# Three attentions with row maxima: the first group's keys and queries are loaded in two halves, and its row scores run by halves

## The reference

```python
scores = jnp.einsum('bhqd,bhkd->bhqk', wq, wk) * scale
scores = jnp.where(mask[None, None], neg, scores)
attn = jax.nn.softmax(scores, axis=-1)
outs.append(jnp.einsum('bhqk,bhkd->bhqd', attn, wv))
```

## Time and profile before

| | us |
|---|---|
| median of 3 runs | 2514.82 (2509.34 to 2515.09) |
| the profiled execution | 2509.64 |
| its span | 2507.9 |
| PE busy | 2108.8 (84%) |
| DVE busy | 1603.6 (64%) |
| ACT busy | 1412.7 (56%) |

### The profile page before, as it was taken

The page is one execution under the profiler, slowest core; times in us unless marked ns, Lnnn a source line. Parts: engine busy times, 40 slices in busy tenths (PEclk is TensorE's granted clock), DMA queues, the critical chain, the costliest instruction groups (busy, mean ns, idle before and its releaser), DMA issues. The chain is left out here.

```text
span 2507.9 us, 37005 instructions
## 1 busy us (share of the span) xinstructions
PE 2108.8 (84%) x13722; PEld 1249.1 (50%) x13732; DVE 1603.6 (64%) x3493; ACT 1412.7 (56%) x2024; POOL 781.3 (31%) x426
## 2 busy tenths in 40 slices
PE   4999999999999935758737786999979746999798
PEld 2666666666666522612323543444446633444367
DVE  5887787887877556631256655877623686877324
ACT  3777776777777643269752343466653152566541
POOL 3787776877877401142101203100000022000000
PEclk8999999999999966879958897799989876999999
DMA  2000000000000050062050211311010003110100
GB/s 75 1 5 1 3 5 1 1 3 5 1 3 1 1 172 0 17 159 53 1 172 1 73 45 46 83 40 40 2 34 1 1 8 90 50 40 21 35 1 18
DMA packets 43908, 82.10 MB, mean 33 GB/s; under 512 B 8962, under 2 KB 17810, under 8 KB 40722
## 3 DMA queue, kind: packets, MB, share of 16 engines
q1 hardware_dynamic: 43730, 79.74, 11.4%
HBM read 64.09 MB, written 14.88 MB: 31 GB/s over the span
## 5 line engine op out<-in xcount | busy, mean ns | idle before, releaser
L800 ACT ACTIVATE probs<-psum_banks 128x1024 f32<-128x1024 f32 (+1 forms) x416 | 381.3, 979 | 249.2 <-PE psum_banks L670 154.0
L1231 POOL TENSOR_SCALAR l0a_rows<-l0a_rows,l0a_rinv 128x1024 f32<-128x1024 f32 x160 | 454.8, 2847 | 188.0 <-DVE l0a_rinv L1193 184.2
L879 DVE TENSOR_REDUCE neg_max<-psum_banks 128x1 f32<-128x512 f32 (+3 forms) x672 | 406.1, 659 | 155.7 <-PE psum_banks L702 96.5
L1181 DVE TENSOR_REDUCE l0a_nmax<-psum_banks 128x1 f32<-128x1024 f32 x256 | 312.5, 1221 | 140.1 <-PE psum_banks L1075 138.2
L1127 ACT ACTIVATE l0a_rows<-psum_banks,l0a_nmax 128x1024 f32<-128x1024 f32 x256 | 286.0, 1117 | 60.6 <-DVE l0a_nmax L1181 59.3
L666 PE MATMUL psum_banks<-q_stack,k_stack 75*128 75x512 bf16 (+7 forms) x1216 | 277.0, 338 | 50.1 <-ACT probs L800 23.7
L698 PE MATMUL psum_banks<-k_stack,q_stack 72*128 72x128 bf16 (+3 forms) x1024 | 246.3, 325 | 46.4 <-DMA q_stack<-q_parts 41.8
L1089 PE MATMUL psum_banks<-packed,l0a_rows 128*128 128x128 f32 x2048 | 267.1, 273 | 2.0 <-POOL l0a_rows L1231 0.9
L1074 PE MATMUL psum_banks<-l0a_kh,l0a_qw 128*128 128x512 f32 x512 | 242.7, 474 | 21.4 <-POOL l0a_qw L1220 13.5
L1089 PEld LDWEIGHTS psum_banks<-packed,l0a_rows 128*128 128x128 f32 x2048 | 239.1, 141 | 42.4 <-issue 4.8
L686 PE MATMUL psum_banks<-probs,v_ones 128*32 128x512 f32 (+3 forms) x2432 | 238.8, 504 | 10.3 <-ACT o_sum L771 6.5
(11 more groups left out here) (289 smaller groups left out, 3516.5 us busy)
## 6 DMA issues: line engine op xcount, KB each, us to landing
q_stack<-q_parts SPq DMA_DIRECT2D x24, 576.0 KB
k_stack<-k_parts SPq DMA_DIRECT2D x48, 192.0 KB
qkv<-in_l0f_w SPq DMA_DIRECT2D x6, 1024.0 KB, 5.6
moe_b<-in_l0f_b SPq DMA_DIRECT2D x32, 128.0 KB, 3.7
k_stack<-k_eight SPq DMA_DIRECT2D x16, 256.0 KB
l1f_w<-in_l1f_w SPq DMA_DIRECT2D x16, 256.0 KB, 4.5
q_stack<-q_parts SPq DMA_DIRECT2D x32, 96.0 KB
q_parts<-parts SPq DMA_DIRECT2D x12, 256.0 KB
```

The lines of the kernel that those rows point to most:

```text
L800: act.activation(S.Pt[:, U % PBUFS, 2 * half:2 * half + 2, c0:HALF], PS[:, bank:bank + 2, c0:HALF], ACT.Exp).then_inc(exp_done, 1)
L879: dve.tensor_reduce(out, scores, AX, ALU.max, negate=True).then_inc(job_read, 1)
L1181: dve.tensor_reduce(R.nmax4[:, s % 4:s % 4 + 1], scores(s), AX, ALU.max, negate=True).then_inc(max_done, 1)
L1231: rows_divided.mark(pool.tensor_scalar(R.Pr[:, s % RING, :], R.Pr[:, s % RING, :], R.rinv4[:, s % 4:s % 4 + 1], None, ALU.mult))
```

## The change

In the three attentions with maxima, group 0 alone is loaded in two halves, heads 0 and 1, then heads 2 and 3: eight transfers of half the size instead of four. The first four count on a new semaphore, `half_landed`, the other four on `loaded`. The rows jobs of group 0 that came first are sorted, stably, so that all of heads 0 and 1 stand ahead of all of heads 2 and 3. The first job waits for `half_landed`; each job of group 0 that starts with head 2 waits for `loaded`. All other groups and all other jobs stay as they are. The whole diff:

```diff
--- before.py
+++ after.py
@@ -476,6 +476,7 @@
 
 def side_jobs(ng, nu, nk, use_max, lead):
 
+
     steps = [[] for _ in range(ng * nu + LAG + 5)]
 
     def spread(events, s0, n):
@@ -486,6 +487,8 @@
         first, second = row_jobs(nk)
         for g in range(ng):
             jobs = [("rows", g, job) for job in first + second]
+            if g == 0:
+                jobs = sorted(jobs[:len(first)], key=lambda e: e[2][1][0] >= 2) + jobs[len(first):]
             whole = ("turn", g, (0, 1))
             s0 = 1 + (g - lead) * nu
             if g >= lead and not second:
@@ -565,10 +568,10 @@
     for U in range(total):
         visits.append(visits[-1] + (1 if narrow(U) else 2))
 
-    with phase(S, 25) as (block, sems):
+    with phase(S, 26) as (block, sems):
         (cols_ready, exp_done, masked, pv_done, evicted, job_ready, job_read, split_done, c_split, c_copied,
          summed, part_done, rest_done, zeroed, v_ready, ones_set, stored) = sems[:17]
-        loaded, c_loaded = sems[17:21], sems[21:25]
+        loaded, c_loaded, half_landed = sems[17:21], sems[21:25], sems[25]
 
         def spare(e, w):
             return PS[:, ring[number[e] % len(ring)], 0:w]
@@ -599,12 +602,14 @@
                     for r0, parts in ((0, 3), (24, 3), (48, 2)):
                         sp.dma_start(S.Qst[64 * i + r0:64 * i + r0 + HD8 * parts, at, :],
                                      S.q_parts[b, 0:parts, :, heads, :].rearrange("j d h t -> (j d) h t")).then_inc(loaded[g % SLOTS], 16)
-                if use_max:
-                    k_rows = short_keys(S, b, keys)[:, :, h0:h0 + 4, :].rearrange("d j h t -> (d j) h t")
-                    q_rows = S.q_parts[b, :, :, h0:h0 + 4, :].rearrange("j d h t -> (j d) h t")
+                for i0, i1 in () if not use_max else ((0, 2), (2, 4)) if g == 0 else ((0, 4),):
+                    landing = half_landed if i1 == 2 else loaded[g % SLOTS]
+                    at, heads = slice(slot(g, i0), slot(g, i1 - 1) + 1), slice(h0 + i0, h0 + i1)
+                    k_rows = short_keys(S, b, keys)[:, :, heads, :].rearrange("d j h t -> (d j) h t")
+                    q_rows = S.q_parts[b, :, :, heads, :].rearrange("j d h t -> (j d) h t")
                     for copy in range(3):
-                        sp.dma_start(S.Kst[24 * copy:24 * (copy + 1), at, :], k_rows).then_inc(loaded[g % SLOTS], 16)
-                    sp.dma_start(S.Qst[0:72, at, :], q_rows.unsqueeze(1).to_broadcast([24, 3, 4, T])).then_inc(loaded[g % SLOTS], 16)
+                        sp.dma_start(S.Kst[24 * copy:24 * (copy + 1), at, :], k_rows).then_inc(landing, 16)
+                    sp.dma_start(S.Qst[0:72, at, :], q_rows.unsqueeze(1).to_broadcast([24, 3, i1 - i0, T])).then_inc(landing, 16)
 
             def load_c(e):
                 k, g, sides = turn_at[e], e[1], e[2]
@@ -690,7 +695,9 @@
 
             def scores(e):
                 _, g, (kind, heads, j) = e
-                if number[e] == 0 or order[number[e] - 1][:2] != ("rows", g):
+                if number[e] == 0:
+                    pe.wait_ge(half_landed, per_group)
+                elif order[number[e] - 1][:2] != ("rows", g) or (g == 0 and heads[0] == 2):
                     pe.wait_ge(loaded[g % SLOTS], per_group * (g // SLOTS + 1))
                 bank = spare(e, HALF)
 
```

## The result

| | before | changed |
|---|---|---|
| median of 8 runs each, us | 2513.0 | 2505.96 |
| lowest and highest | 2509.34, 2517.32 | 2503.04, 2508.49 |
| ratio, with its 95% interval | | 0.9967 [0.9956, 0.9978] |
| profiled execution, span, us | 2507.9 | 2505.2 |

The changed kernel is faster, by 0.33% as the ratio has it (8.3 us; its interval runs from 5.5 to 11 us) and by 7.0 us, 0.28%, between the medians. The time is inside the forecast range, and the gain a little more than the forecast 6.3 us. The 0.3% that I had drawn as the limit of "no change" lies between the two figures.

What follows compares the result with a forecast made beforehand. PE, busy 84%, was taken as the bound, idling at each attention's start for the queries' transfer. Gains of 3.5 us in two causal attentions less 0.7 windowed gave 6.3 us, from 2514.82 to 2508.5, range 2501 to 2515.

Steps and rivals of the forecast that it cites:

- First half in the causal attentions: Start of each causal attention: half the amount lands sooner, so PE starts 3.5 us earlier.
- all move by the same amount: Causal attentions: maxima, turn, shift, group 1's load and first columns move with step 0's jobs; 3.5 us gained each.
- rival 3 of the prediction: Causal attentions, chance 0.1: clock rises only after the next value products, up to 5.6 us more each; 4.9 us slower, 2519.7.
- Second half hidden: Causal attentions: seven jobs of heads 0 and 1, 4.2 us, cover the second half's landing; stall 0 to 0.5 us.
- Rival 4: Start of the attentions, chance 0.08: a stall before heads 2 and 3 loses the whole gain; 2514.8 us.
- rival 1: Group 0's loads, chance 0.2: halves less than half as fast, PE stalls at the eighth job; 3.3 us gained, 2511.5.
- New order free: Group 0's row scores: sorting the same 14 jobs by heads costs 0.
- The windowed attention: First attention: PE starts about 1.5 us earlier, but groups 1 to 3 issue 1.9 us later; cost 0.7 us.
- rival 2: Windowed attention, chance 0.22: group 0's turn comes earlier and loads catch up, gaining 1.5 us there; 8.9 us altogether, 2505.9.
- The sum: Whole kernel: 7.0 us from two causal attentions less 0.7 in the windowed one, 6.3 us, 0.25%.
- The rule weighed: Loads: the skill's fit, 2.0 us plus bytes at 436 GB/s per transfer, gives 1.3 us per causal attention, 1.9 overall.
- the signs that I had named for "wrong": PE waiting over 2 us amid step 0; clock rising elsewhere than after first values; stages after the attentions changing length.

Runs made afterwards that it cites:

- ones last: Changed kernel with the rows of ones issued behind the loads of groups 1 to 3 in the windowed attention; 2503.77 us against 2513.09 before, ratio 0.9956.
- causal, ones last: Changed kernel with halves in the causal attentions alone and the ones issued last in the windowed one; 2505.37 us against 2513.09 before, ratio 0.9967.
- ACT's queue: Changed kernel with the windowed attention's groups 1 to 3 issued from ACT's queue instead of behind group 0 on SP's; 2503.7 us against 2512.62 before, ratio 0.9958.
- keys whole: Changed kernel, windowed attention only: ones issued behind groups 1 to 3, group 0's keys whole, only its queries halved; 2504.43 us against 2513.09 before, ratio 0.9962.

## Why the prediction held, point by point

**First half in the causal attentions: right, a little small.** Forecast 3.5 us each, bounds 2.5 and 3.7. The lengths of the second attention's stage (to the mixture weights), and how much earlier than before PE starts in it:

| kernel | earlier start | shorter stage |
|---|---|---|
| changed | 4.37 | 4.17 |
| changed, again | 4.77 | 4.69 |
| causal only | 3.53 | 3.54 |
| causal only, again | 4.13 | 3.85 |
| ones last | 4.20 | 4.25 |
| causal, ones last | 4.19 | 3.79 |
| ACT's queue | 4.33 | 4.42 |
| keys whole | 1.88 | 1.06 |
| halves without the order | 4.54 | 1.32 |

The stage shrinks by what PE starts earlier, to within 0.4 us in all but the last two rows. The step "all move by the same amount" was right, and the last row is the exception that I had named: without the new order the start is as early and the gain is gone.

What the stage follows in every row is the rise of the clock. It comes 47.2 us after the first load before the change, 42.5 to 43.8 in the first seven rows, 47.0 with the keys whole and 46.0 without the order. In all 22 causal stages without a fall, halved or not, the stage is 238.9 to 240.3 us longer than the time to the rise. With the keys whole the first value product came 1.9 us earlier than before (43.50 for 45.40), but the clock still rose at 47.0, and of 1.88 us 1.06 were left. So the gain depends on the rise moving with the start, as rival 3 of the prediction has it; with halves and the new order it did in all but this row. In the third attention the six profiles without a fall of the clock are 3.45 to 4.14 us shorter with PE 3.46 to 4.27 earlier. Over all 14 stages with halves, the new order and no fall the mean is 3.7 us; with the two falls counted in, it is 3.0. The bound of 3.7 was too low: ten of the 16 stages started earlier by more. The starts scatter, from 5.5 to 6.8 us and once 8.43, and I could not see that from one profile of before, whose two starts lie 0.3 us apart.

**Second half hidden: right.** Forecast landing about 10.2 us after the first issue and at most 0.5 us of stall. It lands at 9.63 and 10.34 in the kernel that waits for it, and at the eighth job of the changed kernel there is no wait. Rival 4 and rival 1, which had a stall there, fell.

**New order free: right.** 286.99 and 286.65, against 286.97 and 286.63.

**The windowed attention: right in kind and place.** PE starts after 5.17 us (forecast 5.5), waits for group 1 until 1423.82 (forecast 1422.9 to 1423.9), the shift isn't earlier, and rival 2 fell with that. Forecast cost 0.7 us, bounds -1.5 and +1.9. At the first columns it is 20.54, 20.77 and 21.18 in three profiles with halves, mean 20.83, against 20.18, 19.78, 20.39, 20.06 and 20.36 in five without, mean 20.15: 0.7 us. The whole stage costs a little more: 139.78, 139.63 and 140.96, mean 140.1, against 139.11, 138.44, 139.28, 139.02 and 139.35, mean 139.0. For the other 0.4 there is a candidate that I had not foreseen. During the wait for group 1 the granted clock falls. The timeline has PE idle for 2.95 us until 1423.82, and in the windows of the changed kernel shown above the clock is at 1.00 in 1421 to 1422, at 0.71 in the next microsecond, at 0.50 when PE starts again, and still there in 1428 to 1429. The earlier trace rows had 1.00 in both of its microseconds. In the five profiles without halves the clock didn't fall at this place. In the three with halves it was down for 6.8, 3.4 and 10.2 us, in the last two from 0.9 and 1.8 us after the wait for group 1 had ended. That the fall is worth the 0.4 us is argued from these rows, not shown by a run, and the wait need not be its cause: with the ones last and no halves the clock fell without such a wait. The loads indeed end later, as forecast: 183 GB/s still flow in 1428 to 1429, where the earlier trace rows had 8 a microsecond earlier.

**The sum.** Forecast 2 x 3.5 - 0.7 = 6.3. By stages it is 2 x 3.7 - 1.1 = 6.3, and 2 x 4.1 - 1.1 = 7.1 if the second attention's mean without the one odd row stands for both. With the two falls counted in, it is only 2 x 3.0 - 1.1 = 4.9. The medians say 7.0 and, when the changed kernel was run again, 5.95. The term that was a little small was the half of the load: 3.5 forecast, 3.7 to 4.1 measured. The median of before that I had set the sum against, 2514.82 from three runs, was 1.8 us above the 2513.0 of eight, which made 2508.5 that much too high. With that, 2505.96 lies just outside the 2506.9 to 2510.3 that I had given to my own mechanism, and on the 2505.9 of rival 2, whose mechanism the traces refute. That is chance; the gain of 7.0 is inside my 4.5 to 7.9.

**The rule weighed.** The halves land at 5.9 and 9.6 us, so the estimate by the Trainium skill (DMA: Bandwidth & Descriptors, "Anatomy of one DMA — SWDGE (gpsimd) path"), 1.3 us gained per causal attention, isn't borne out: 3.7 were. The fit stands in that section, and not in the one that I named; it was made for transfers issued from GpSimd, where these are issued from SP. The advice to batch transfers (the same page, "Bandwidth") the measurements do bear out one step further: in three parts the same 1180 KB took 12.04 and 11.75 us instead of 9.63 and 10.34.

**Rival 3, the clock: it happened, but not as I had put it.** I thought that the rise was tied to the first value products, and that it might come later. In 14 of 16 causal stages with halves and the new order it rose at 42.5 to 47 us after the first load, once the first value product had begun, as it did in the eight without halves or without the new order (46 to 48.6). In the other two, the third attention of the changed kernel's first profile and of the second run of the causal-only one, it rose at 39.3, in the midst of row scores; this is one of the signs that I had named for "wrong". That helps for a moment: the value product takes 1.71 us instead of 2.3 to 3.2. Then PE is ahead of the second side's shift, whose four transfers are still being issued (3.31 us from 2109.93), waits 1.66 us (1.34 in the other), and the clock is at half for the next 17 us. The net price is some 5.4 us in that attention. It is in none of those eight stages. Two in 16 against none in 8 is no proof that the change causes it, but the second attention of the kernel in three parts did the same: a rise at 40.2 us, a wait of 1.31, a fall at 47.1. What brings the early rise about stays open: in both cases PE started 6.8 us after the first load, but it did so in one other stage (6.78) as well, which had no fall.

**The one profile.** Its span shrank by just 2.7 us. By its stages the edit gave 6.7 (4.17 in the second attention and the 3.24 by which the third began earlier, less 0.67 in the first), the fall of the clock took 5.4 back, the stage between the second and the third attention gave 2.57, and the first and the last stage took 1.1. The third of these terms is the other sign that I had named for "wrong", and it stays open. That stage has two lengths: 236.4 to 236.7 in six profiles, 239.0 to 240.0 in seven. In the short ones the clock rises at 160 and at 218 us of the stage, in the long ones at 163 to 164 and 224 to 225. All three kernels that load the causal groups whole have the long one, of the eight profiles with halves and the new order only three; the means are 239.4 and 237.6. If that belongs to the change, the sum of 4.9 with the falls becomes 6.8, as near to the medians as the 6.3. Three profiles don't decide it, so the timed gain is not shown to come from the starts of the attentions alone.

No version beats the changed kernel by more than the intervals allow. Causal halves only (0.9977 and 0.9960) would spare the windowed attention's 1.1 us and aren't told apart from it.

## What to carry to other kernels

When a phase begins with a load that nothing hides, cut it so that the first piece is as small as the work behind it can cover the rest, and reorder the work by pieces; here seven jobs of 4.2 us cover a second half that is 3.1 to 3.9 us behind the first. Cutting alone moved the wait to the second job, and a third cut delayed the last part by more than the start came earlier. The time saved ahead of the rise of the clock was kept here only where the rise moved too. Every load that stands behind the cut one on the same queues pays: look whether somebody wants it early, as group 1 did in the windowed attention. To judge a change of this size, compare the lengths of stages over several profiles, not two spans.

## What the runs showed of the hardware

- After PE's waits of 2.95 us and 1.66 us for a transfer the clock was at 0.50 (1.2 GHz). In the first attention it fell within the wait and was back after 6.8 us; in the third it fell some 0.9 us after it and stayed down for 17 us, though PE was then busy all the time (12.50 of 12.50 us). The second fall cost some 5.4 us. The wait isn't shown to be the cause: in the kernel with three parts the clock fell with no idle time over 0.21 us ahead of an instruction.
- Through step 0 of a causal attention the clock stayed at 0.50, with PE busy 5.69 of 8 us in 2084 to 2092 and 2.00 of 2 us in the row scores of 2077 to 2079. In most stages it rose within the first 16 f32 value matmuls, in two of 16 ahead of them.
- The load of 1180 KB on 72 partitions, whole or in halves, ran at 141 to 203 GB/s in windows of 2 to 4 us once it was under way; over the first 4 us it ran at 131 GB/s in halves and at 75 in three parts (second attention).
- Issuing the loads of groups 1 to 3 up to 6.3 us earlier from a second queue brought group 1's only 1.6 us earlier.
